# Low-rank delta of the conditioning weight: made in products of 512 columns, partly at the start, and brought back through DRAM

## The chip, the cores and the metric

One core of one Trainium2 chip. The metric is the time of one execution on the device in microseconds (us); lower is better. All data is float32.

## What is computed

The input x has 4096 tokens (32 tiles of 128) of 2048 features. Cut to what matters:

```python
lora_delta = lora_B @ lora_A * 0.5                     # [2048, 64] @ [64, 2048]
cb = codebook / max(|codebook|); scale = exp(scale_log)  # one scale per 128 inputs
normalized = (weight + lora_delta).reshape(O, I // 128, 128) / scale
idx = searchsorted((cb[:-1] + cb[1:]) * 0.5, normalized)  # codebook of 32
w_eff = (cb[idx] * scale).reshape(O, I) + lora_delta
cond = x @ w_eff.T
ffn = cond @ W_base.T + b_base + 2 * mixed(cond) @ B_w.T   # mixed: 8 experts of rank 16, softmax routing
out = x + ffn
```

## The kernel before

**Tiling.** The kernel multiplies the two big weights first: for each block b of 128 input features (16 of them) it makes the row block of G = w_eff.T @ [W_base, A_w, router_w].T, adds the identity, and then multiplies x by G. The width is 2072 columns, cut in five chunks (384, 384, 384, 512, 408). Blocks come in groups of 2, 3, 4, 4 and 3. A group g has two stages: weights(g), which makes its rows of G in 80 slots (for group 0 this is the startup), and tokens(g), 32 tiles of x by five chunks, summed over groups in DRAM (part). The last group also does the routing and the output.

**Quantizing.** A weight block is done in two halves of 1024 output features, so q = 0 to 31, with b = q // 2 and h = q % 2. For each q: POOL adds the delta to the raw weight and divides by the scale (normalise, L924 and L927). Of the 31 thresholds, 25 are units: ACT makes a mask (L678), DVE adds it times its step (L814); six are spare ones (ACT L688, POOL L938 and L942). DVE's L818 closes the sum, POOL's effective(q) multiplies by the scale and adds the delta again (L947, L949). Later ACT and POOL split the result in a high and a low part (L694, L953).

**The order.** All five engines run the same list of events, walk(). An engine does its part of an event and goes on; it is held only by semaphores, and works strictly in order. units(q) yields ("unit", q, j) for j = 0 to 24. In startup() after j = 7 comes ("rows", q - 1) for q = 1 to 4: PE multiplies the half block q - 1 by eight row tiles of the wide weight (L528, plain float32, two records for a product), and SP loads the row tiles, three ahead (L379). ("x_first", 0) comes after j = 12 of q = 4. tokens_of() and weights_of() interleave the units of later q with chunks and slots: q = 5 to 9 in tokens(0), 10 and 11 in weights(1), 12 to 17 in tokens(1), 18 and 19 in weights(2), 20 to 25 in tokens(2), 26 and 27 in weights(3), 28 to 31 in tokens(3).

**The delta.** lora_B is in SBUF (lb), lora_A comes by 128 columns (la, SP, L374). delta(q, r) makes half of a half block: four products of 128 columns into the four quarters of the one PSUM bank pd (L508), and ACT copies the bank to dl, times 0.5 (L668). PE does delta(q + 1, 0) at j = 3 and delta(q + 1, 1) at j = 6 of q; ACT copies at j = 5 and j = 8. Each product waits until the copy of the last one is done. The two of q = 0 stand ahead of the walk on both engines.

Of the kernel before, what the change touches and what calls it, by code (L numbers as in the profile page):

```python
# [49 lines left out]
PER_RING = tuple(len(range(r, NS, RING)) for r in range(RING))  # L50
HOME = (2, 2, 0, 0, 1, 1)
RELEASED = (NS - 4, NS - 2, NS)

COMPUTE = (
# [4 lines left out]
)  # L59
LOADS = (  # L60
    "sl", "lb", "cb", "id", "la0", "la1", *(f"w{r}" for r in range(RAW)), "r0", "r1", "r2",
    *(f"k{r}" for r in range(RING)), "x0", "x1", "x2", "pi0", "pi1", "pi2", "po0", "po1", "po2", "os0", "os1", "os2",
    "bw", "bb", "cr",
)
# [90 lines left out]
class Room:  # L155
    def __init__(self, nc, ctx):
        self.nc = nc
        self.top = -(-nc.sbuf_base // 32) * 32
        raw = [self.space(H * 4) for _ in range(RAW)]
        self.wr = [self.put(f"wr{r}", at, H) for r, at in enumerate(raw)]  # L160
        self.wl = [self.put(f"wl{r}", at, H, F32R) for r, at in enumerate(raw)]
        self.wh = [self.take(f"wh{r}", H, F32R) for r in range(HIGH)]
        self.gh = [self.take(f"gh{k}", DX, F32R) for k in range(NMAX)]
        self.gl = [self.take(f"gl{k}", DX, F32R) for k in range(NMAX)]
        at_x = [self.space(NMAX * 512) for _ in range(3)]
        self.xw = [self.put(f"xw{p}", at, NMAX * 128) for p, at in enumerate(at_x)]
        self.xl = [self.put(f"xl{p}", at, NMAX * 128, F32R) for p, at in enumerate(at_x)]
        self.xh = [self.take(f"xh{p}", NMAX * 128, F32R) for p in range(3)]
        at_p = [self.space(DX * 4) for _ in range(3)]
        self.part = [self.put(f"part{p}", at, DX) for p, at in enumerate(at_p)]  # L170
        self.rows = [self.put(f"rows{p}", at, DX) for p, at in enumerate(at_p)]
        at_k = [at_p[HOME[r]] + (r % 2) * 4096 for r in range(RING)]
        self.kw = [self.put(f"kw{r}", at, 512) for r, at in enumerate(at_k)]
        self.kl = [self.put(f"kl{r}", at, 512, F32R) for r, at in enumerate(at_k)]
        self.kh = [self.put(f"kh{r}", at + 2048, 512, F32R) for r, at in enumerate(at_k)]
        at_dl = self.top
        self.dl = [self.take(f"dl{k}", H) for k in range(2)]
        at_pp = self.top
        self.pp = self.take("pp", H)
        self.tm = self.take("tm", H)  # L180
        self.mk = [self.take(f"mk{k}", H, U8) for k in range(NM)]
        self.mp = [self.take(f"mp{k}", H, U8) for k in range(2)]
        at_lb = self.top
        self.lb = self.take("lb", H)
        self.la = [self.take(f"la{k}", 128) for k in range(2)]
        self.sc = self.take("sc", NB * NB)
        self.rs = self.take("rs", NB * NB)
        self.idn = self.take("idn", 128)
        self.cb = self.take("cb", NC)
        self.cn = self.take("cn", NC)  # L190
        self.u = self.take("u", NC + 1)
        self.th = self.take("th", NJ)
        self.bj = self.take("bj", NJ)
        self.dj = self.take("dj", NJ)
        self.sm = self.take("sm", 2)
        assert self.top <= nc.sbuf_usable_end

        self.tmp = self.put("tmp", at_x[0], 1536)
        self.bw = self.put("bw", at_dl, D)
        self.bs = self.put("bs", at_pp, D, F32R, 96)  # L200
        self.sa = [self.put(f"sa{k}", at_lb + 512 * k, 128, F32R, 96) for k in range(3)]
        self.z = self.put("z", at_lb + 1536, 128)
        self.zt = self.put("zt", at_lb + 2048, 128)
        self.cr = self.put("cr", at_lb + 2560, 96)
        self.ex = self.put("ex", at_lb + 2944, NE)
        self.pe = self.put("pe", at_lb + 2976, NE)
        self.st = self.put("st", at_lb + 3008, 4)

        def bank(name, n=1):
            return ctx.enter_context(nc.psum_tensor(name, [128, n * 512], F32))[:]  # L210

        self.acc = bank("acc", 2)
        self.pd = bank("pd")
        self.m = [bank(f"m{c}") for c in range(NCH)]
        self.pz, self.pm, self.p5 = self.acc[:, 0:512], self.acc[:, 512:1024], self.pd
# [45 lines left out]
def wait_evacuated(e, S, g, t, c):  # L261
    if g == 0 and c in ACT_CHUNKS:
        e.wait_ge(S["ea"], len(ACT_CHUNKS) * t + ACT_CHUNKS.index(c) + 1)
    elif g == 0:
        e.wait_ge(S["ed"], len(DVE_CHUNKS) * t + DVE_CHUNKS.index(c) + 1)
    else:
        e.wait_ge(S["ed"], len(DVE_CHUNKS) * NT + NCH * NT * (g - 1) + NCH * t + c + 1)


def raw_of(q):  # L270
# [90 lines left out]
BOOK_READY = 23  # L361


def sync_program(e, R, S, io, part, out):
    def raw(q):
        b, h = q // 2, q % 2
        if q >= RAW:
            wait_consumed(e, S, q - RAW)
        e.dma_start(R.wr[raw_of(q)], io["w"][b][:, h * H:(h + 1) * H]).then_inc(S[f"w{raw_of(q)}"], 16)

    def lora(b):
        if b >= 2:
            e.wait_ge(S["pd"], 4 * (b - 1))
        e.dma_start(R.la[b % 2], io["la"][:, b * 128:(b + 1) * 128]).then_inc(S[f"la{b % 2}"], 16)  # L374

    def row(r):
        if r >= 3:
            e.wait_ge(S["row"], r - 2)
        e.dma_start(R.rows[r % 3], io["wb"][r % NB]).then_inc(S[f"r{r % 3}"], 16)  # L379
# [42 lines left out]
    e.dma_start(R.cb, io["cb"].partition_broadcast(128)).then_inc(S["cb"], 16)  # L422
    raw(0)
    raw(1)
    lora(1)
    e.dma_start(R.idn, io["id"]).then_inc(S["id"], 16)
    for q in range(2, 2 * N0 + 1):
        raw(q)
    for r in range(3):
        row(r)  # L430
    for ev in walk():
        what, at = ev[0], ev[1:]
        if what == "unit":
            q, j = at
            if j == 0 and 2 * N0 < q + 1 < NQ:
                raw(q + 1)
            if j == 12 and q % 2 == 0 and 2 <= q < NQ - 2:
                lora(q // 2 + 1)
        elif what == "rows":
            for r in range(8 * at[0] + 3, min(8 * at[0] + 11, NB * N0)):  # L440
                row(r)
# [53 lines left out]


def tensor_program(e, R, S):
    def delta(q, r):
        b, h = q // 2, q % 2
        n = 2 * q + r  # L500
        if n == 0:
            e.wait_ge(S["lb"], 16)
        if h == r == 0:
            e.wait_ge(S[f"la{b % 2}"], 16 * (b // 2 + 1))
        if n:
            e.wait_ge(S["dl"], n)
        for k in range(4):
            done = e.matmul(R.pd[:, k * 128:(k + 1) * 128], R.lb[64 * h:64 * h + 64, (4 * r + k) * 128:(4 * r + k + 1) * 128],  # L508
                            R.la[b % 2][64 * h:64 * h + 64, :], start=True, stop=True)
        done.then_inc(S["pd"], 1)  # L510

    def own(b, c):
        return CUT[c] <= b * 128 < CUT[c + 1]
# [100 lines left out]
    def rest(t):  # L614
        if t:
            e.wait_ge(S["e5"], t)
        else:
            e.wait_ge(S["dl"], 2 * NQ)
        low(R.p5, t, NCH - 1, True).then_inc(S["m5"], 1)

    def turn(t):
# [12 lines left out]
            e.wait_ge(S["cr"], 48)  # L634
        e.matmul(R.pm[0:96, 0:128], R.cr, R.zt, start=True, stop=True).then_inc(S["pm"], 1)

    delta(0, 0)
    delta(0, 1)
    for ev in walk():
        what, at = ev[0], ev[1:]  # L640
        if what == "unit":
            q, j = at
            if q + 1 < NQ and j in (3, 6):
                delta(q + 1, (j - 3) // 3)
        elif what == "rows":
            rows(*at)
        elif what == "slot":
            slot(*at)
        elif what == "chunk":
            chunk(*at)  # L650
        elif what == "route":
            route(*at)
        elif what == "turn":
            turn(*at)
        elif what == "mix":
            mix(*at)
        elif what == "last":
            last(*at)
        elif what == "rest":
            rest(*at)  # L660


def scalar_program(e, R, S):
    def delta(q, r):
        e.wait_ge(S["pd"], 2 * q + r + 1)
        if q >= 2 and r == 0:
            e.wait_ge(S["we"], q - 1)
        e.activation(R.dl[q % 2][:, r * 512:(r + 1) * 512], R.pd, ACT.Copy, scale=0.5).then_inc(S["dl"], 1)  # L668

    def unit(q, j):  # L670
        k, w = NV * q + j, R.wr[raw_of(q)]
# [78 lines left out]
        for k in (0, 32, 64):  # L750
            e.activation(R.sa[t % 3][k:k + NR, :], R.pm[k:k + NR, 0:128], ACT.Copy).then_inc(S["mh"], 1)

    delta(0, 0)
    delta(0, 1)
    for ev in walk():
        what, at = ev[0], ev[1:]
        if what == "unit":
            q, j = at
            unit(q, j)
            if q + 1 < NQ and j in (5, 8):  # L760
                delta(q + 1, (j - 5) // 3)
        elif what == "rows_out":
            rows_out(*at)
        elif what == "split":
# [36 lines left out]
def vector_program(e, R, S):  # L801
# [73 lines left out]
    for ev in walk():  # L875
# [19 lines left out]
        elif what == "split" and at[0] == NQ - 1:  # L895
            e.wait_ge(S["we"], NQ)
            e.memset(R.bw, 0.0).then_inc(S["bw0"], 1)
            e.wait_ge(S["pd"], 2 * NQ)
            e.memset(R.cr, 0.0).then_inc(S["cr0"], 1)
        elif what == "slot" and at == (LAST, 20):  # L900
            e.wait_ge(S["bshi"], 1)
# [15 lines left out]
def gpsimd_program(e, R, S):  # L917
    def normalise(q):
        w, d = R.wr[raw_of(q)], R.dl[q % 2]
        e.wait_ge(S[f"w{raw_of(q)}"], 16 * (q // RAW + 1))  # L920
        for r in range(2):
            part = slice(512 * r, 512 * r + 512)
            e.wait_ge(S["dl"], 2 * q + r + 1)
            e.tensor_tensor(w[:, part], w[:, part], d[:, part], ALU.add).then_inc(S["wg"], 1)  # L924
        e.wait_ge(S["wg"], 2 * q + 2)
        e.wait_ge(S["es"], SCALE_FIRST if q < 2 else SCALE_READY)
# [39 lines left out]
                        ALU.subtract).then_inc(S["xl"], 1)  # L966

    def clear():
        e.wait_ge(S["pd"], 2 * NQ)
        for k in range(3):  # L970
            e.memset(R.sa[k].bitcast(F32), 1.0).then_inc(S["s1"], 1)
        e.wait_ge(S["s1"], 3)
# [41 lines left out]

def build(nc, io, out):
    part = nc.dram_tensor("part", [NT, 128, DX], F32, kind="Internal").ap()
    with ExitStack() as ctx:
        R = Room(nc, ctx)
        S = {name: ctx.enter_context(nc.semaphore(f"s_{name}")) for name in COMPUTE}
        S.update({name: ctx.enter_context(nc.semaphore(f"d_{name}")) for name in LOADS})  # L1020
        with nc.Block() as block:
            @block.sync
            def _(e):
                sync_program(e, R, S, io, part, out)

            @block.scalar
            def _(e):
# [45 lines left out]
```

## Time and profile before

| | |
|---|---|
| median of 3 runs | 2537.79 us (2536.51 to 2541.07) |
| the profiled execution | 2540.63 us, span 2538.8 us |
| granted TensorE clock, mean | 0.981 |
| DMA | 461.64 MB, mean 182 GB/s |

The profile is of one execution; times in it count from the start of its span. PE is the matmul part of TensorE and PEld its weight load, DVE VectorE, ACT ScalarE, POOL GpSimd, SP the queue that issues DMAs. A row of a timeline gives the start, the duration, the engine, the line, the operation, output and inputs, and in brackets the idle time of the engine before it and what ended it. L508 is line 508 of the kernel.

### The profile page before, as it was taken

The numbers are of one execution on the slowest core, as the hardware profiler recorded it, in microseconds if no ns is written. First come the engines' busy times: TensorE is split into PE (matmuls) and PEld (weight loads), VectorE is DVE, ScalarE is ACT, GpSimd is POOL, SyncE is SP. The second block draws the span as 40 slices with busy tenths as digits, with TensorE's granted clock in tenths as the row PEclk, the third lists the DMA queues.
The fourth block names the chain that finished last, engine by engine and source line by source line (L and its number), as shares of the span: only waits on it lengthen the run. The fifth ranks groups of instructions, "written<-read, shape, count | busy, mean of one in ns | idle before, by whom it ended". The sixth has DMA issues, their size and how long they took to land.

```text
span 2538.8 us, 32166 instructions
## 1 busy us (share of the span) xinstructions
PE 2371.1 (93%) x12160; PEld 2176.6 (86%) x12160; DVE 1560.8 (61%) x1960; ACT 1499.9 (59%) x1902; POOL 1523.9 (60%) x1062
## 2 busy tenths in 40 slices
PE   1887888889999999999999999999999989999999
PEld 1445777878999989899999989899999989899998
DVE  7996999544899964347777744435566631044444
ACT  6996999666888856666666636654445414311111
POOL 4875888688687877866666646864444436501010
PEclk9988999989999999999999999999999999999999
DMA  2563454434677753345555642335555544456665
GB/s 105 199 213 123 176 184 163 164 100 124 225 285 265 275 210 88 103 140 212 210 213 208 218 151 86 103 125 210 214 215 208 210 156 131 154 199 236 237 236 200
DMA packets 123375, 461.64 MB, mean 182 GB/s; under 512 B 14242, under 2 KB 61602, under 8 KB 82210
## 3 DMA queue, kind: packets, MB, share of 16 engines
q1 hardware_dynamic: 123220, 459.59, 51.6%
q8 instruction: 96, 1.57, 0.2%
q14 instruction: 59, 0.48, 0.1%
HBM read 290.19 MB, written 169.35 MB: 181 GB/s over the span
## 4 chain that ended last, share of the span: by engine, by line
PE 75%; DVE 10%; POOL 7%; ACT 3%; issue 3%; DMA 2%; SPq 0%; DVEq 0%; POOLq 0%; ACTq 0%
PE m L571 17%; PE m L572 17%; PE m L573 17%; DVE acc L814 8%; PE m L555 7%; PE m L557 7%; PE m L556 7%; PE pd L508 2%; ACT mk L678 2%; POOL pp L942 1%; DMA kw<-in_wb 1%; POOL tm L938 1%; PE m L601 1%; POOL kl L959 1%; ACT mp L688 1%
## 5 line engine op out<-in xcount | busy, mean ns | idle before, releaser
L814 DVE SCALAR_TENSOR_TENSOR acc<-mk,dj,acc 128x1024 f32<-128x1024 uint8 x800 | 1026.4, 1283 | 340.6 <-ACT mk L678 229.0
L678 ACT ACTIVATE mk<-wr,bj 128x1024 uint8<-128x1024 f32 x800 | 904.0, 1142 | 233.4 <-DVE acc L814 219.1
L571 PE MATMUL m<-gh,xh 128*128 128x384 f32 (+2 forms) x2560 | 912.8, 357 | 45.7 <-POOL xl L965 19.1
L572 PE MATMUL m<-gl,xh 128*128 128x384 f32 (+2 forms) x2560 | 903.0, 353 | 0.0
L573 PE MATMUL m<-gh,xl 128*128 128x384 f32 (+2 forms) x2560 | 900.7, 352 | 0.0
L571 PEld LDWEIGHTS m<-gh,xh 128*128 128x128 f32 x2560 | 484.4, 189 | 80.1 <-POOL xl L965 23.7
L573 PEld LDWEIGHTS m<-gh,xl 128*128 128x128 f32 x2560 | 484.1, 189 | 23.2
L572 PEld LDWEIGHTS m<-gl,xh 128*128 128x128 f32 x2560 | 484.8, 189 | 20.3
L555 PE MATMUL m<-kh,wh 128*128 128x384 f32 (+2 forms) x1120 | 402.5, 359 | 40.5 <-POOL kl L959 35.3
L959 POOL TENSOR_TENSOR kl<-kw,kh 128x384 fp32r<-128x384 f32 (+2 forms) x320 | 340.7, 1085 | 165.9 <-ACT kh L699 165.4
L836 DVE TENSOR_TENSOR part<-m,part 128x384 f32<-128x384 f32 (+2 forms) x480 | 280.5, 586 | 242.7 <-PE m L573 242.1
L557 PE MATMUL m<-kh,wl 128*128 128x384 f32 (+2 forms) x1120 | 397.4, 355 | 0.0
L556 PE MATMUL m<-kl,wh 128*128 128x384 f32 (+2 forms) x1120 | 397.2, 355 | 0.0
L942 POOL TENSOR_TENSOR pp<-pp,tm 128x1024 f32<-128x1024 f32 x160 | 383.2, 2395 | 13.4
L965 POOL TENSOR_TENSOR xl<-xw,xh 128x384 fp32r<-128x384 f32 (+2 forms) x160 | 171.3, 1072 | 350.4 <-ACT xh L719 349.6
L699 ACT ACTIVATE kh<-kw 128x384 fp32r<-128x384 f32 (+2 forms) x320 | 172.4, 546 | 318.3 <-DMA kw<-in_wb 317.1
L938 POOL TENSOR_SCALAR tm<-mp,dj 128x1024 f32<-128x1024 uint8 x192 | 215.4, 1122 | 173.5 <-ACT mp L688 169.4
L555 PEld LDWEIGHTS m<-kh,wh 128*128 128x128 f32 x1120 | 214.6, 192 | 58.7 <-POOL kl L959 40.8
L556 PEld LDWEIGHTS m<-kl,wh 128*128 128x128 f32 x1120 | 214.5, 192 | 9.7
L557 PEld LDWEIGHTS m<-kh,wl 128*128 128x128 f32 x1120 | 214.1, 191 | 9.8
L688 ACT ACTIVATE mp<-wr,bj 128x1024 uint8<-128x1024 f32 x192 | 217.9, 1135 | 0.0
L822 DVE TENSOR_TENSOR gl<-m,gh 128x384 fp32r<-128x384 f32 (+2 forms) x80 | 45.2, 588 | 203.3 <-ACT gh L714 203.3
(84 smaller groups left out, 1479.9 us busy)
## 6 DMA issues: line engine op xcount, KB each, us to landing
part<-part SPq DMA_DIRECT2D x256, 1036.0 KB, 4.8
kw<-in_wb SPq DMA_DIRECT2D x192, 192.0 KB, 2.4
rows<-in_wb SPq DMA_DIRECT2D x32, 1036.0 KB, 4.8
out<-part SPq DMA_DIRECT2D x32, 1024.0 KB, 3.9
wr<-in_w SPq DMA_DIRECT2D x32, 512.0 KB, 5.8
kw<-in_wb SPq DMA_DIRECT2D x64, 256.0 KB, 2.6
xw<-in_x SPq DMA_DIRECT2D x64, 256.0 KB, 2.9
kw<-in_wb SPq DMA_DIRECT2D x64, 204.0 KB, 2.4
```

The lines of the kernel that those rows point to most:

```text
L555: e.matmul(bank[:, 0:w], high, kh, start=t == 0, stop=False)
L556: e.matmul(bank[:, 0:w], high, kl, start=False, stop=False)
L557: done = e.matmul(bank[:, 0:w], low, kh, start=False, stop=t == NB - 1 and not own(b, c))
L571: e.matmul(R.m[c][:, 0:w], xh, gh, start=k == 0, stop=False)
L572: e.matmul(R.m[c][:, 0:w], xh, gl, start=False, stop=False)
L573: done = e.matmul(R.m[c][:, 0:w], xl, gh, start=False, stop=stop and k == n - 1)
L678: e.activation(R.mk[k % NM], w, ACT.Identity, bias=R.bj[:, j:j + 1], scale=GROW).then_inc(S["mk"], 1)
L688: e.activation(R.mp[k % 2], w, ACT.Identity, bias=R.bj[:, NV + i:NV + i + 1], scale=GROW).then_inc(S["mp"], 1)
L814: e.scalar_tensor_tensor(R.acc, R.mk[k % NM], R.dj[:, j:j + 1], R.acc, ALU.mult, ALU.add).then_inc(S["ac"], 1)
L836: e.tensor_tensor(p, R.m[c][:, 0:width(c)], p, ALU.add).then_inc(S["ed"], 1)
L942: e.tensor_tensor(R.pp, R.pp if i else w, R.tm, ALU.add).then_inc(S["pp"], 1)
L959: e.tensor_tensor(R.kl[r][:, 0:w], R.kw[r][:, 0:w], R.kh[r][:, 0:w].bitcast(F32), ALU.subtract).then_inc(S["gl"], 1)
```

## The change

The delta is no longer made half by half just ahead of its use. A product is now 512 columns wide: delta(n) multiplies one tile of 128 output features of lb by four blocks of lora_A, n = 0 to 63. Its result spans four blocks, so ACT copies it into one of two buffers ds, two products side by side, and SP stores each pair to a DRAM tensor delta (512 KB, runs of 1 KB). SP loads the half block that q + 1 needs at j = 5 of q into dl, and POOL waits for that load. Ahead of the walk PE and ACT do four direct products of the old form (q = 0 and 1) and then delta(0) to delta(15). The other 48 are placed at j = 2, 8, 14 and 20 of q = 1 to 12, on PE and ACT in the same event; from q = 13 on there are none. la and ds lie in space of gh3 and gl3, which only groups of four blocks use.

```diff
+DIRECT = 4
+QUADS = NB // 4
+DU_AT = (2, 8, 14, 20)
...
+def early(q):
+
+    first = 16 + len(DU_AT) * (q - 1)
+    return range(first, first + len(DU_AT)) if 0 < q and first < 16 * QUADS else ()
...
+    def lora(Q):
+        if Q >= 2:
+            e.wait_ge(S["pd"], DIRECT + 16 * (Q - 1))
+        e.dma_start(R.la[Q % 2], io["la"][:, Q * 512:(Q + 1) * 512]).then_inc(S[f"la{Q % 2}"], 16)
...
+    def delta_out(n):
+        Q, ot, p = n // 16, n % 16, n // 2 % 2
+        e.wait_ge(S["dl"], DIRECT + n + 1)
+        e.dma_start(delta[4 * Q:4 * Q + 4, :, (ot - 1) * 128:(ot + 1) * 128].rearrange("b p i -> p b i"),
+                    R.ds[p].rearrange("p (b i) -> p b i", b=4)).then_inc(S[f"ds{p}"], 16)
...
+    def delta_in(q):
+        b, h = q // 2, q % 2
+        pairs = 8 * (b // 4) + 4 * h + 4
+        for p in range(2):
+            e.wait_ge(S[f"ds{p}"], 16 * (pairs // 2))
+        e.wait_ge(S["we"], q - 1)
+        e.dma_start(R.dl[q % 2], delta[b, :, h * H:(h + 1) * H]).then_inc(S[f"dq{q % 2}"], 16)
...
+    lora(1)
+    for n in range(1, 16, 2):
+        delta_out(n)
+    lora(2)
...
+            if j in DU_AT and early(q):
+                n = early(q)[DU_AT.index(j)]
+                if n % 2:
+                    delta_out(n)
+                if n % 16 == 15 and n // 16 + 2 < QUADS:
+                    lora(n // 16 + 2)
+            if j == 5 and 1 <= q < NQ - 1:
+                delta_in(q + 1)
...
+    def direct(h, r):
+        if h == r == 0:
             e.wait_ge(S["lb"], 16)
-        if h == r == 0:
-            e.wait_ge(S[f"la{b % 2}"], 16 * (b // 2 + 1))
...
+            e.wait_ge(S["la0"], 16)
+        else:
+            e.wait_ge(S["dl"], 2 * h + r)
...
         done.then_inc(S["pd"], 1)
...
+    def delta(n):
+        Q, h, ot = n // 16, n % 16 // 8, n % 8 * 128
+        if n % 16 == 0:
+            e.wait_ge(S[f"la{Q % 2}"], 16 * (Q // 2 + 1))
+        e.wait_ge(S["dl"], DIRECT + n)
+        e.matmul(R.pd, R.lb[64 * h:64 * h + 64, ot:ot + 128], R.la[Q % 2][64 * h:64 * h + 64, :],
+                 start=True, stop=True).then_inc(S["pd"], 1)
...
-    delta(0, 0)
-    delta(0, 1)
+    for n in range(DIRECT):
+        direct(n // 2, n % 2)
+    for n in range(16):
+        delta(n)
...
-            if q + 1 < NQ and j in (3, 6):
-                delta(q + 1, (j - 3) // 3)
+            if j in DU_AT and early(q):
+                delta(early(q)[DU_AT.index(j)])
...
+    def delta(n):
+        p, ot = n // 2 % 2, n % 2 * 128
+        e.wait_ge(S["pd"], DIRECT + n + 1)
+        if n >= 4 and n % 2 == 0:
+            e.wait_ge(S[f"ds{p}"], 16 * (n // 4))
+        e.activation(R.ds[p].rearrange("p (b i) -> p b i", b=4)[:, :, ot:ot + 128],
+                     R.pd.rearrange("p (b i) -> p b i", b=4), ACT.Copy, scale=0.5).then_inc(S["dl"], 1)
...
-            if q + 1 < NQ and j in (5, 8):
-                delta(q + 1, (j - 5) // 3)
+            if j in DU_AT and early(q):
+                delta(early(q)[DU_AT.index(j)])
...
-            e.wait_ge(S["dl"], 2 * q + r + 1)
+            if q < 2:
+                e.wait_ge(S["dl"], 2 * q + r + 1)
+            elif r == 0:
+                e.wait_ge(S[f"dq{q % 2}"], 16 * (q // 2))
...
+    delta = nc.dram_tensor("delta", [NB, 128, D], F32, kind="Internal").ap()
```

In the diff, the functions with lora and delta_out, delta_in are SP's; of the two functions delta(n) the first is PE's and the second ACT's.

## Rows read from the trace of the kernel before

**Rows 1.** The page: busy time of each engine, and the chain by engine.
```profile
PE 2371.1 (93%) x12160; PEld 2176.6 (86%) x12160; DVE 1560.8 (61%) x1960; ACT 1499.9 (59%) x1902; POOL 1523.9 (60%) x1062
PE 75%; DVE 10%; POOL 7%; ACT 3%; issue 3%; DMA 2%; SPq 0%; DVEq 0%; POOLq 0%; ACTq 0%
```

**Rows 2.** The chain by line: 1100 to 1500 us, then 230 to 470.
```profile
by line: PE m L571 30.8%; PE m L572 30.3%; PE m L573 30.0%; PE pd L508 3.3%; PE m L557 1.9%; PE m L556 1.9%; PE m L555 1.9%
...
by line: DVE acc L814 17.3%; issue 14.9%; ACT mk L678 7.4%; POOL pp L942 6.2%; PE m L571 5.9%; PE m L573 4.9%; PE m L572 4.8%; POOL tm L938 4.6%; POOL xl L965 4.3%; POOL wr L924 4.2%; POOL wl L953 4.0%; POOL wr L949 4.0%; DVE wr L818 3.2%; 
```

**Rows 3.** Busy time by stretch, length, PE, PEld, DVE, ACT, POOL, clock, DMA: tokens(0), (2), (1).
```profile
324.40:369.00 44.60, 39.04 (x196) 35.56 (x196) 41.43 (x45) 41.98 (x54) 36.30 (x24) 0.96 0.47 173
...
1242.00:1301.10 59.10, 59.10 (x318) 55.66 (x317) 45.59 (x52) 39.52 (x40) 38.49 (x23) 1.00 0.59 213
691.40:735.80 44.40, 44.05 (x238) 41.01 (x237) 43.58 (x52) 38.71 (x40) 37.03 (x23) 1.00 0.72 273
```

**Rows 4.** Timeline of DVE, startup: the ends of q = 0, 1, 3, 4.
```profile
25.75 34.72 DVE L814 SCALAR_TENSOR_TENSOR acc<-mk,dj,acc 128x1024 f32<-128x1024 uint8 x25 [4.82 <-ACT acc L682]
60.50 1.28 DVE L818 SCALAR_TENSOR_TENSOR wr<-acc,cn,pp 128x1024 f32<-128x1024 f32 x1
...
97.69 1.28 DVE L818 SCALAR_TENSOR_TENSOR wr<-acc,cn,pp 128x1024 f32<-128x1024 f32 x1
...
174.35 1.28 DVE L818 SCALAR_TENSOR_TENSOR wr<-acc,cn,pp 128x1024 f32<-128x1024 f32 x1
...
211.96 1.29 DVE L814 SCALAR_TENSOR_TENSOR acc<-mk,dj,acc 128x1024 f32<-128x1024 uint8 x1 [17.16 <-ACT mk L678]
...
229.29 1.28 DVE L818 SCALAR_TENSOR_TENSOR wr<-acc,cn,pp 128x1024 f32<-128x1024 f32 x1
```

**Rows 5.** Timeline of PE: a delta half at the high clock, rows(1), rows(3).
```profile
102.88 1.16 PE L508 MATMUL pd<-la,lb 64*128 64x128 f32 x8
...
107.47 29.61 PE L528 MATMUL m<-rows,wr 128*128 128x384 f32 x80
...
184.93 30.13 PE L528 MATMUL m<-rows,wr 128*128 128x384 f32 x80
```

**Rows 6.** Timeline of ACT: a delta half is copied, q = 2.
```profile
105.63 0.58 ACT L668 ACTIVATE dl<-pd 128x512 f32<-128x512 f32 x1
```

**Rows 7.** Timeline of ACT: before the first unit.
```profile
10.07 0.60 ACT L668 ACTIVATE dl<-pd 128x512 f32<-128x512 f32 x1 [2.16 <-PE pd L508]
21.49 1.15 ACT L678 ACTIVATE mk<-wr,bj 128x1024 uint8<-128x1024 f32 x1 [10.82 <-POOL wr L927]
```

**Rows 8.** Timeline of all engines: the first delta products on PE.
```profile
5.23 2.04 PE L508 MATMUL pd<-la,lb 64*128 64x128 f32 x8 [5.23 <-DMA la<-in_la]
...
7.96 2.07 PE L508 MATMUL pd<-la,lb 64*128 64x128 f32 x8 [0.69 <-ACT dl L668]
```

**Rows 9.** Groups of PE by form: 73 to 77 us, 77.7 to 80.5 us.
```profile
L528 PE MATMUL m<-rows,wr 128*128 128x512 f32 x2 | 1.7, 956 | 0.0
...
L528 PE MATMUL m<-rows,wr 128*128 128x512 f32 x2 | 1.0, 592 | 0.0
```

**Rows 10.** Stretches of two delta products; PEclk is the third number from the end.
```profile
182.90:185.00 2.10, 2.07 (x9) 1.85 (x9) 2.00 (x2) 2.05 (x2) 1.86 (x2) 0.50 0.11 39
...
102.90:104.00 1.10, 1.10 (x9) 0.94 (x8) 1.08 (x1) 1.10 (x2) 1.10 (x2) 1.00 0.97 301
```

**Rows 11.** The page: loads of raw weight, KB each, median us to landing.
```profile
wr<-in_w SPq DMA_DIRECT2D x32, 512.0 KB, 5.8
```

**Rows 12.** Timeline of POOL: the end of effective(1).
```profile
101.03 2.36 POOL L949 TENSOR_TENSOR wr<-wr,dl 128x1024 f32<-128x1024 f32 x1
```

**Rows 13.** Waits of ACT, 230 to 470 us: us in total, times, longest.
```profile
ACT part L725 <- PE m L573: 27.0, 16, 7.3
```

**Rows 14.** Waits, from 470 us on.
```profile
ACT dl L668 <- PE pd L508: 42.1, 17, 5.1
```

**Rows 15.** Groups, 640 to 2070 us: the delta products.
```profile
L508 PE MATMUL pd<-la,lb 64*128 64x128 f32 x304 | 44.8, 289 | 0.0
```

More of the change, by code:

```diff
@@ L60 @@
 LOADS = (
-    "sl", "lb", "cb", "id", "la0", "la1", *(f"w{r}" for r in range(RAW)), "r0", "r1", "r2",
+    "sl", "lb", "cb", "id", "la0", "la1", "ds0", "ds1", "dq0", "dq1", *(f"w{r}" for r in range(RAW)), "r0", "r1", "r2",
     *(f"k{r}" for r in range(RING)), "x0", "x1", "x2", "pi0", "pi1", "pi2", "po0", "po1", "po2", "os0", "os1", "os2",
@@ L163, in __init__ @@
         self.gh = [self.take(f"gh{k}", DX, F32R) for k in range(NMAX)]
+        at_gh, at_gl = self.top - DX * 4, self.top + (NMAX - 1) * DX * 4
         self.gl = [self.take(f"gl{k}", DX, F32R) for k in range(NMAX)]
+        self.la = [self.put(f"la{k}", at_gh + 2048 * k, 512) for k in range(2)]
+        self.ds = [self.put(f"ds{k}", at_gl + 4096 * k, H) for k in range(2)]
         at_x = [self.space(NMAX * 512) for _ in range(3)]
@@ L184, in __init__ @@
         self.lb = self.take("lb", H)
-        self.la = [self.take(f"la{k}", 128) for k in range(2)]
         self.sc = self.take("sc", NB * NB)
@@ L361, with sync_program @@
 BOOK_READY = 23
-def sync_program(e, R, S, io, part, out):
+def sync_program(e, R, S, io, part, delta, out):
     def raw(q):
@@ L369, in raw @@
         e.dma_start(R.wr[raw_of(q)], io["w"][b][:, h * H:(h + 1) * H]).then_inc(S[f"w{raw_of(q)}"], 16)
[L371 to L374, printed above, removed]
+    def lora(Q):
[14 more added lines that the diff above has]
+        e.dma_start(R.dl[q % 2], delta[b, :, h * H:(h + 1) * H]).then_inc(S[f"dq{q % 2}"], 16)
     def row(r):
@@ L424, in sync_program @@
     raw(1)
-    lora(1)
     e.dma_start(R.idn, io["id"]).then_inc(S["id"], 16)
@@ L436, in sync_program @@
                 raw(q + 1)
-            if j == 12 and q % 2 == 0 and 2 <= q < NQ - 2:
-                lora(q // 2 + 1)
+            if j in DU_AT and early(q):
[6 more added lines that the diff above has]
+                delta_in(q + 1)
         elif what == "rows":
@@ L497, in tensor_program @@
 def tensor_program(e, R, S):
[L498 to L501, printed above, removed]
+    def direct(h, r):
+        if h == r == 0:
             e.wait_ge(S["lb"], 16)
-        if h == r == 0:
-            e.wait_ge(S[f"la{b % 2}"], 16 * (b // 2 + 1))
-        if n:
-            e.wait_ge(S["dl"], n)
+            e.wait_ge(S["la0"], 16)
+        else:
+            e.wait_ge(S["dl"], 2 * h + r)
         for k in range(4):
-            done = e.matmul(R.pd[:, k * 128:(k + 1) * 128], R.lb[64 * h:64 * h + 64, (4 * r + k) * 128:(4 * r + k + 1) * 128],
-                            R.la[b % 2][64 * h:64 * h + 64, :], start=True, stop=True)
+            ot = (4 * r + k) * 128
+            done = e.matmul(R.pd[:, k * 128:(k + 1) * 128], R.lb[64 * h:64 * h + 64, ot:ot + 128],
+                            R.la[0][64 * h:64 * h + 64, 0:128], start=True, stop=True)
         done.then_inc(S["pd"], 1)
+    def delta(n):
[5 more added lines that the diff above has]
+                 start=True, stop=True).then_inc(S["pd"], 1)
     def own(b, c):
@@ L617, in rest @@
         else:
-            e.wait_ge(S["dl"], 2 * NQ)
+            e.wait_ge(S["dl"], DIRECT + 16 * QUADS)
         low(R.p5, t, NCH - 1, True).then_inc(S["m5"], 1)
@@ L663, in scalar_program, with direct @@
 def scalar_program(e, R, S):
[L664 to L668, printed above, removed]
+    def direct(h, r):
+        e.wait_ge(S["pd"], 2 * h + r + 1)
+        e.activation(R.dl[h][:, r * 512:(r + 1) * 512], R.pd, ACT.Copy, scale=0.5).then_inc(S["dl"], 1)
+    def delta(n):
[5 more added lines that the diff above has]
+                     R.pd.rearrange("p (b i) -> p b i", b=4), ACT.Copy, scale=0.5).then_inc(S["dl"], 1)
     def unit(q, j):
@@ L751, in mix @@
             e.activation(R.sa[t % 3][k:k + NR, :], R.pm[k:k + NR, 0:128], ACT.Copy).then_inc(S["mh"], 1)
-    delta(0, 0)
-    delta(0, 1)
+    for n in range(DIRECT):
+        direct(n // 2, n % 2)
+    for n in range(16):
+        delta(n)
     for ev in walk():
@@ L897, in vector_program @@
             e.memset(R.bw, 0.0).then_inc(S["bw0"], 1)
-            e.wait_ge(S["pd"], 2 * NQ)
+            e.wait_ge(S["pd"], DIRECT + 16 * QUADS)
             e.memset(R.cr, 0.0).then_inc(S["cr0"], 1)
@@ L968, in clear @@
     def clear():
-        e.wait_ge(S["pd"], 2 * NQ)
+        e.wait_ge(S["pd"], DIRECT + 16 * QUADS)
         for k in range(3):
@@ L1023, in _ @@
             def _(e):
-                sync_program(e, R, S, io, part, out)
+                sync_program(e, R, S, io, part, delta, out)
             @block.scalar
```

## Prediction, made before the changed kernel was run

> **What bounds the kernel now.** I read the page first. TensorE (PE) is busy 93% of the span and holds 75% of the chain that ended last; DVE, ACT and POOL stand near 60% each [rows 1]. Such shares average over stages, so I then asked for the chain by stretch. From 1100 to 1500 us it is PE and nothing else, 3.3% of it the delta products of L508; but from 230 to 470 us, the tokens of group 0, the quantizing of the weights leads (DVE L814, ACT L678, POOL) and PE has a small part [rows 2]. Busy times by stretch say the same: PE 59.1 of 59.1 us in one q of tokens(2), 44.05 of 44.4 in tokens(1) with DVE at 43.58, and in group 0 DVE 41.4, ACT 42.0 and PE 39.0 of 44.6 [rows 3]. The kernel thus has two parts. Up to about 470 us the chain of units decides: ACT makes the mask, DVE adds it. Later PE decides. PE works in program order, so a delay of the first part moves the end one to one, while PE time saved later comes off the end.
>
> Startup is the stretch to look at. DVE ends its q with L818. The ends for q = 0, 1, 3 and 4 (start plus 1.28) are 61.8, 99.0, 175.6 and 230.6 us [rows 4]: q = 1 took 37.2, q = 2 and 3 together 76.6, q = 4 55.0. The 25 units of q = 0 take 34.7 us [rows 4], 1.39 each. The long last one has a wait of 17.2 us on ACT [rows 4], which stood at j = 12 for the first x tile: in its list SP has that load behind the row loads, and these wait for PE. Meanwhile PE does rows(q-1), eight row tiles that need about 30 us: 29.6 and 30.1 us in two of the four passes [rows 5]. They run beside the units, because nothing that ACT needs during a q is queued behind them: both delta products of a q stand ahead (j = 3 and 6; rows at j = 7), and ACT picks them up two units later.
>
> **The change, part by part.**
>
> (a) Ahead of the first unit. Before, ACT needed only two evacuations, and from 10.7 us sat idle for 10.8 us until the scales were ready and its first mask began at 21.5 us [rows 7]. Now 4 direct and 16 wide products come first, each one waiting for the evacuation of the last since there is a single bank, pd. A direct one has the old form: products start at 5.2 and 8.0 us, one each 2.75 us [rows 8]; four end at 5.2 + 11.0 = 16.2. A wide one is two records of 512 columns. No row shows it for delta; the nearest is the row product of 512 columns in two records: a mean of 956 ns at the low clock and 592 at the high one [rows 9], so 1.9 or 1.2 us. The hand-over costs 0.7 us, the idle time of PE between products [rows 8]. A wide product thus takes 2.6 or 1.9 us. Which clock? The granted clock is not recorded that early, but eight narrow records take 2.04 us there, as at a granted 0.50 (1.2 GHz), against 1.16 us at 1.00 (2.4 GHz) [rows 5, 8, 10]. PE stayed low while busy three quarters of the time over the products shown, and the wide ones keep it as busy, so I take 2.6: 16 x 2.6 = 41.6, and ACT is free at 57.8 instead of 21.5, +36 us. At the high clock it is 16 x 1.9 = 30.4, end 46.6, +25. The stores: a ds buffer is needed again three products after its store goes out, 3 x 2.6 - 0.6 = 7.2 us; the nearest row for 512 KB is 5.8 us to landing [rows 11]. Just hidden; at the high clock it has 5.1 us and would hold the chain back, so +25 to +45 is the range. The ends of (a) lie on the chain whole: DVE and POOL have nothing else to do.
>
> By the Trainium skill, TensorE: Matmul & The Clock Gate, section "What's actually happening", the clock follows how busy the array has been of late, and sustained work brings it to 2.4 GHz. Read strictly, forty microseconds of this would rise and (a) would be the +25 case, the sum 11 us less; the products of rows 8 do not show it.
>
> (b) The wait that is new. DU_AT puts deltas at j = 2, 8, 14, 20, on PE and on ACT in the same event. In startup rows(q-1) is yielded after j = 7, so PE does the delta of j = 8 after all eight row tiles, and ACT, in order, cannot make the mask of j = 9 until it has evacuated that delta. Behind it stand DVE's units 9 to 24, POOL's spares and normalise(q+1), and so the next q. Let T be the end of L818 of q-1. effective(q-1) ends at T + 4.4 (101.03 + 2.36 against 99.0) [rows 12], the rows take 30 us, to T + 34.5; the product at the high clock 1.1, the evacuation 0.6 [rows 6], the mask 1.1 [rows 7]: T + 37.3. Then 16 units x 1.39 = 22.3 and L818 1.3: T + 61. Four periods (q = 1 to 4) of 61 are 244 against 168.8 (230.6 - 61.8): **+75 us**. Within it the x stall of q = 4 is gone: SP's row loads and the load of x are done by T + 43, about when ACT comes to j = 12. In SP's queue delta_in at j = 5 waits for effective(q-1), T + 4.4, ahead of the row loads of j = 7, the first of which needs a row product done at T + 10: no cost. delta_out of j = 8 waits there until T + 37, and only x stands behind it. Bounds: 65 (rows take 28) to 82 (rows slowed by the other loads, ACT with its six spare masks behind for a few us).
>
> (c) Group 0, q = 5 to 9. Four evacuations per q instead of two: 10 more x 0.5 = 5 us of an ACT that is 94% busy. Also 20 waits at PE's heels, since the two-unit lead is gone. The nearest row is ACT's wait for PE at L725: 16 times, 27.0 us, 1.7 each [rows 13]; 20 x 1.7 = 34 is the upper end, nothing the lower. PE is mostly level with ACT here, so I take a quarter, about 10: **+15**, 0 to 39.
>
> (d) q = 10 to 12, 12 products in the same event. ACT's waits for delta after 470 us: 17 times, 42.1 us [rows 14], 2.5 each, upper end 30; most is slack. SP's delta_out stands ahead of kw loads in weights(1), with three slots of lead. **+7**, 0 to 30.
>
> (e) q = 13 on: no products and no evacuations. PE spends 44.8 us on 304 records from 640 us on [rows 15], 38 halves of 1.18 each; 36 of them go, 42.5 us. In tokens(2) and (3) all of it is on the chain; in tokens(1), 10 halves, DVE stands within 1 us of PE per q [rows 3], so about half goes: **-35**, from -42 to -25.
>
> (f) DMA: 16.8 MB more written, about 15.7 MB more read on 462. delta_in goes out at j = 5 and POOL needs it at j = 9: over 5.6 us against 5.8 [rows 11], but in group 0 and later POOL reaches normalise later still, and in startup the stall of (b) covers it. Lost cover would cost 1 to 2 us per q. Zero.
>
> Sum: 36 + 75 + 15 + 7 - 35 = **+98 us**. The profiled execution took 2540.6 us (span 2538.8); 2638.6. The median of the runs is 2.8 lower: **2636**.
>
> **The rivals.**
> 1. As forecast, both ACT stalls real. Lowest: 25 + 65 + 0 + 0 - 42 = +48 (2586); highest 45 + 82 + 39 + 30 - 25 = +171 (2709). 88%; its middle 2590 to 2695.
> 2. The new waits reach much further: each delta store or delta_in blocks SP's order and starves kw, x or part in the groups, one more stall of about 2.5 us for each of the 48 placed products: +120 on top, 2756. For it: one queue, waits on other engines in it. Against: loads run two tiles or three slots ahead. 5%.
> 3. The startup stall of (b) is not there, because PE gets the j = 8 product done before the rows: then the sum is 98 - 75 = +23, 2559. Against: PE is in order and the product is behind the rows in its list. 3%.
> 4. Faster: stall absent as in 3, prologue at the high clock (+25), group 0 and weights(1) absorb the rest at nothing, all of L508 gained: 25 - 42 = -17, 2521. It decides for faster if rows(q-1) are over by about T + 15, when ACT comes to j = 8, so in some 10 us; they take 30 [rows 5]. 3%.
> 5. That the change does little: the two sides cancel within 0.2%, 5 us. 1%.
>
> **How the numbers follow.** Faster 0.03, same 0.01, slower 0.96. A measurement of this kernel tells 0.2% from no change. The range 2590 to 2695 leaves out rivals 2 to 5 and the far ends of the first.
>
> **What would show it.** Right: first mask of ACT near 58 us; in q = 1 to 4 an idle time of ACT of about 20 us before the second wide evacuation, ended by PE's delta product, with rows just ahead of it; DVE's L818 about 61 us apart; group 0 beginning its tokens about 110 us later; q from 13 on about 2.2 us shorter in tokens(2). Wrong: rows that end before ACT's j = 8, or a prologue under 45 us; or SP waits that end after the loads are due in weights(1).

## The result: slower by 4.8%

The changed kernel takes 2661.5 us (median of 4 runs, 2652.8 to 2666.5) against 2538.6 of the kernel before on the same chip: a ratio of 1.048, 95% interval 1.0451 to 1.0509. The forecast was 2636. The profiled execution took 2660.9 us, its span is 2659.1, which is 120.3 longer than before.

The page of the changed kernel, to be set beside [rows 1]; then its waits from 814 to 1065 us, where q = 13 to 17 lie (us in total, times, longest):

```profile
PE 2396.6 (90%) x11808; PEld 2144.1 (81%) x11808; DVE 1563.8 (59%) x1960; ACT 1500.2 (56%) x1906; POOL 1524.0 (57%) x1062
PE 71%; POOL 7%; ACT 7%; DVE 6%; DMA 6%; issue 2%; SPq 0%; DVEq 0%; POOLq 0%; ACTq 0%
...
ACT xh L767 <- DMA xw<-in_x: 59.8, 23, 4.5
...
POOL wr L977 <- DMA dl<-delta: 20.9, 5, 4.9
```

DMA has 6% of the chain where it had 2%. All shares say little until the span is cut at the ends of the q. The table does that: each number is the distance, in one trace, between two ends of DVE's closing instruction (L818 before, L868 after; as in [rows 4]). "mask" is the start of ACT's first mask, "tail" what follows the end of q = 31.

| us | mask | q0 | q1-3 | q4 | q5-9 | q10-12 | q13-17 | q18-31 | tail | span |
|---|---|---|---|---|---|---|---|---|---|---|
| before | 21.5 | 40.3 | 113.9 | 54.9 | 228.1 | 232.7 | 222.6 | 1132.3 | 492.6 | 2538.8 |
| after | 61.3 | 40.3 | 187.6 | 61.5 | 229.3 | 234.6 | 248.7 | 1099.6 | 496.2 | 2659.1 |
| e1 | 61.2 | 40.3 | 120.4 | 58.2 | 232.3 | 231.3 | 250.0 | 1094.0 | 496.4 | 2584.2 |
| e2 | 38.7 | 40.3 | 188.7 | 61.6 | 229.4 | 234.7 | 247.3 | 1096.2 | 495.5 | 2632.3 |
| e3 | 60.9 | 40.3 | 189.8 | 61.7 | 229.3 | 237.2 | 238.4 | 1097.2 | 495.9 | 2650.8 |
| e4 | 21.6 | 40.3 | 113.8 | 53.5 | 227.8 | 233.0 | 233.4 | 1131.3 | 492.7 | 2547.4 |
| e5 | 61.0 | 40.3 | 120.0 | 58.1 | 232.8 | 232.9 | 222.4 | 1096.0 | 496.2 | 2559.4 |
| e6 | 22.2 | 40.3 | 113.8 | 54.6 | 231.6 | 234.5 | 256.4 | 1097.4 | 497.0 | 2547.8 |
| e7 | 22.6 | 40.3 | 113.8 | 54.8 | 231.6 | 234.6 | 230.6 | 1097.1 | 493.7 | 2519.1 |
| e8 | 21.8 | 40.3 | 113.9 | 54.7 | 227.6 | 233.3 | 222.6 | 1131.3 | 495.7 | 2541.2 |
| e9 | 24.6 | 40.3 | 113.8 | 54.7 | 234.3 | 235.0 | 223.1 | 1097.1 | 497.0 | 2520.0 |

The first two lines hold the result: +39.8 ahead of the first mask, +73.7 and +6.6 in q = 1 to 4, nearly nothing in q = 5 to 12, +26.1 in q = 13 to 17, -32.7 from q = 18 on, +3.6 in the tail.

**Ahead of the first mask.** ACT in the changed kernel: start, duration, operation, idle before it.

```profile
8.31 0.60 ACT L708 ACTIVATE dl<-pd 128x512 f32<-128x512 f32 x1 [6.29 <-PE pd L540]
...
22.17 0.60 ACT L715 ACTIVATE ds<-pd 128x512 f32<-128x512 f32 x1 [2.16 <-PE pd L549]
24.93 0.60 ACT L715 ACTIVATE ds<-pd 128x512 f32<-128x512 f32 x1 [2.16 <-PE pd L549]
...
60.79 0.60 ACT L715 ACTIVATE ds<-pd 128x512 f32<-128x512 f32 x1 [2.16 <-PE pd L549]
61.29 1.14 ACT L726 ACTIVATE mk<-wr,bj 128x1024 uint8<-128x1024 f32 x1
```

The copies come 2.76 us apart to the last, and the first mask stands right behind the twentieth. PE gives the other half, a direct product (eight narrow records) and a wide one:

```profile
14.48 2.07 PE L540 MATMUL pd<-la,lb 64*128 64x128 f32 x8 [0.69 <-ACT dl L708]
...
20.06 2.07 PE L549 MATMUL pd<-la,lb 64*128 64x512 f32 x2 [0.69 <-ACT ds L715]
```

**The stall in startup.** PE, ACT and DVE in q = 1 of the changed kernel, and the next end:

```profile
106.04 29.71 PE L568 MATMUL m<-rows,wr 128*128 128x384 f32 x80 [42.46 <-POOL wr L1002]
135.68 1.12 PE L549 MATMUL pd<-la,lb 64*128 64x512 f32 x2
...
111.03 1.15 ACT L726 ACTIVATE mk<-wr,bj 128x1024 uint8<-128x1024 f32 x1 [0.24 <-DVE acc L864]
136.84 0.60 ACT L715 ACTIVATE ds<-pd 128x512 f32<-128x512 f32 x1 [24.66 <-PE pd L549]
137.34 1.14 ACT L726 ACTIVATE mk<-wr,bj 128x1024 uint8<-128x1024 f32 x1
...
100.30 1.28 DVE L868 SCALAR_TENSOR_TENSOR wr<-acc,cn,pp 128x1024 f32<-128x1024 f32 x1
...
161.40 1.28 DVE L868 SCALAR_TENSOR_TENSOR wr<-acc,cn,pp 128x1024 f32<-128x1024 f32 x1
```

To be read in this order: all 80 row records are on PE ahead of the product of j = 8; ACT made the mask of that j at 111.0 and then stood 24.7 us; q = 1 took 61.1 us.

### The profile page after: what moved, and what is told of

It reads as the page before. It is cut to its first block, busy times and chain, and to the rows that moved or that the text cites. A ratio compares the mean times of both kernels' runs of the same rounds, so it can differ in the third digit from the quotient of the medians.

```text
span 2659.1 us, 31535 instructions
## 1 busy us (share of the span) xinstructions
PE 2396.6 (90%) x11808; PEld 2144.1 (81%) x11808; DVE 1563.8 (59%) x1960; ACT 1500.2 (56%) x1906; POOL 1524.0 (57%) x1062
## 4 chain that ended last, share of the span: by engine, by line
PE 71%; POOL 7%; ACT 7%; DVE 6%; DMA 6%; issue 2%; SPq 0%; DVEq 0%; POOLq 0%; ACTq 0%
PE m L611 14%; PE m L612 14%; PE m L613 14%; PE m L595 7%; PE m L597 6%; PE m L596 6%; DVE acc L864 5%; PE m L568 4%; DMA part<-part 4%; ACT mk L726 3%; PE pd L549 2%; POOL pp L995 2%; ACT mp L736 1%; POOL kl L1012 1%; POOL tm L991 1%
## 5 line engine op out<-in xcount | busy, mean ns | idle before, releaser
L611 PEld LDWEIGHTS m<-gh,xh 128*128 128x128 f32 x2560 | 486.5, 190 | 120.4 <-POOL xl L1018 45.6
L568 PE MATMUL m<-rows,wr 128*128 128x384 f32 (+2 forms) x320 | 118.8, 535 | 79.7 <-POOL wr L1002 64.5
```

The lines of the kernel that those rows point to most:

```text
L611: e.matmul(R.m[c][:, 0:w], xh, gh, start=k == 0, stop=False)
```

## Experiments

### e1: the products ahead of the rows

```diff
-DU_AT = (2, 8, 14, 20)
+DU_AT = (1, 3, 5, 7)
```

> The changed kernel with its four placed products at j = 1, 3, 5 and 7 instead of 2, 8, 14 and 20: all ahead of the row tiles on PE, nothing else. My theory (ACT is held at j = 8 because PE has the product behind rows(q-1)): ACT's waits of 20 to 26 us for L549 in q = 1 to 4 go, PE now needs about 10 us of paced products and 30 of rows for a q, so L868 comes every 41 us or so in q = 1 to 3 instead of 61 to 65, and q = 4 gets back part of its wait for x (55 to 60). Sum for q = 1 to 4 near 180 instead of 249, the time about 2660 - 68 = 2592. Rival (the stall comes from the traffic or the waits of the stores and loads through DRAM, which stay the same): the periods stay at 61 and the time within 5 us of 2660. Nothing changes for q = 13 to 17 by either.

Measured: 2585.5 us (4 runs, ratio to before 1.0178, 1.0161 to 1.0195), 76 us less than the changed kernel. q = 1 to 4 take 178.6 us. PE in q = 1 of e1:

```profile
109.46 2.07 PE L549 MATMUL pd<-la,lb 64*128 64x512 f32 x2 [0.69 <-ACT ds L715]
111.46 30.39 PE L568 MATMUL m<-rows,wr 128*128 128x384 f32 x80
141.78 1.12 PE L549 MATMUL pd<-la,lb 64*128 64x512 f32 x2
```

The traffic through DRAM is the same, only the place in PE's list is another, and the periods of 61 to 65 us of q = 1 to 3 become 37 to 43. ACT's longest wait for a product in startup falls from 26.3 us to 3.9. The stall came from the order. In q = 4 a wait of 18.5 us for the first x tile is back, as expected in part. What is left in q = 2 and 3 (40.3 and 42.9 instead of 37.2 and 39.5) is PE, as expected: paced products plus 30 us of rows.

### e2: half the prologue

```diff
+AHEAD_OF_WALK = 8
+DU_FIRST = (1, 4, 7, 10, 13, 16, 19, 22)
...
-    for n in range(16):
+    for n in range(AHEAD_OF_WALK):
         delta(n)
...
+    if q == 0:
+        return range(AHEAD_OF_WALK, 16)
```

> The changed kernel with 8 wide products ahead of the walk instead of 16; products 8 to 15 stand in q = 0 at j = 1, 4, 7, 10, 13, 16, 19 and 22. My theory (the prologue lies on the chain whole, 2.76 us for a product at the low clock): the first mask comes at 61.3 - 8 x 2.76 = 39.2 us; in q = 0 ACT has 8 x 0.5 = 4 us more to do and PE is idle, so the end of q = 0 falls from 101.6 to 80 to 84, and the time by 18 to 22 us to about 2640. Rival (the stores of the pairs pace it, not PE and ACT): the products left take longer each, or delta_in of q = 2 lands too late, and less than 10 us are gained.

Measured: 2634.0 us (ratio 1.0371, 1.0352 to 1.0389), 27.6 less than the changed kernel by the medians, 26.8 by the spans, more than the 18 to 22 expected. The first mask comes at 38.7, 22.6 earlier, and q = 0 takes 40.3 us as ever: the eight copies moved there cost nothing, where I had allowed 4 us for them: the copies fit beside DVE's units, which set the pace of q = 0. The prologue is on the chain whole and the stores don't pace it. The other 4 us lie in q = 13 to 19 (-5.0) and are no more than runs of the changed kernel differ by.

### e3 and e4: what makes q = 13 to 17 slow

e3 leaves out the return of the delta from q = 13 on; POOL adds what dl still holds. e4 is the kernel before with an extra load. Both are single runs.

```diff
-            if j == 5 and 1 <= q < NQ - 1:
+            if j == 5 and 1 <= q < 12:
                 delta_in(q + 1)
...
-            elif r == 0:
+            elif r == 0 and q <= 12:
```

```diff
+            if j == 5 and 12 <= q < 17:
+                if q > 12:
+                    e.wait_ge(S["xt"], 16 * (q - 12))
+                e.dma_start(R.xt, io["w"][0][:, 0:H]).then_inc(S["xt"], 16)
```

> The changed kernel without the loads of the delta for the half blocks 13 to 31: POOL adds what dl holds then, so the weights from q = 13 on are not the right ones; all other work is the same. Theory A (the 512 KB read per q, in SP's list and on the DMA queues, is what makes q = 13 to 17 in tokens(1) 49 to 51 us long instead of 44.5): their sum falls from 248.8 to 222 to 230 us. Theory B (SP fell behind during q = 12, where delta stores and loads come together, and the loop of store, part and x loads cannot catch up): the sum stays above 240, since x loads stay late. In tokens(2) and weights(2) and (3) neither expects more than 3 us.

> The kernel before with one extra load of 512 KB into an unused place for each of q = 12 to 16, at j = 5, where the changed kernel has its load of the delta; nobody reads it. Theory A (the extra read alone tips tokens(1)): q = 13 to 17 take 235 to 250 us instead of 222.5, with ACT waiting for x. Theory B (the seed lies in q = 12's delta stores and products, or in POOL's wait for the load): 222 to 226 us, and the time stays within 5 us of 2540.

Measured: in e3 q = 13 to 17 take 238.4 us, between the two forecasts: q = 13 44.5, the rest 47.6 to 50.2, though not one byte of delta is read there. In e4 they take 233.4, again between the forecasts: 44.5, 44.5, 45.6, 49.4, 49.4. The last extra load of e4 goes out in q = 16, and q = 17 is still slow. Neither theory holds alone. The 512 KB load can start it: it is all that e4 adds to the kernel before. In e3 it starts without that load, some 20 us after the last delta store of q = 12. What starts it there is not isolated: e3 still has the four products, their copies and the two stores of q = 12, and, like the changed kernel, no products behind them. Once started it goes on without any of these to the end of q = 17, for 23 tiles in e3 and 6 in e4. ACT waits for x tiles 59.8 us in q = 13 to 17 of the changed kernel, 46.2 in e3 and 28.9 in e4, and in the kernel before not at all. SP in tokens(1), the kernel before, where L412 stores part, L407 loads it and L398 loads x; then e4 near its end (L414, L409, L400), where no extra load is in flight:

```profile
736.42 0.32 SPq L412 DMA_DIRECT2D part<-part  x1
740.32 0.32 SPq L407 DMA_DIRECT2D part<-part  x1
...
741.85 0.33 SPq L398 DMA_DIRECT2D xw<-in_x  x1
745.62 0.33 SPq L412 DMA_DIRECT2D part<-part  x1
```

```profile
867.04 0.33 SPq L409 DMA_DIRECT2D part<-part  x1
867.42 0.43 SPq L400 DMA_DIRECT2D xw<-in_x  x1
868.02 0.32 SPq L414 DMA_DIRECT2D part<-part  x1
876.33 0.32 SPq L409 DMA_DIRECT2D part<-part  x1
```

Before, the store goes out 3.8 us after the x load and the next part load follows it by 3.9 us, which is when the store has landed. In e4 all three go out within a microsecond and SP then stands 8.3 us for the store, which has 1 MB of part and the x tile ahead of it. The x tile of the next load is late by that, PE by the x tile. An estimate from these rows says why the lag is not made up: 8.3 us for the store and 1.0 for the three issues are 9.3 us for a tile, where 44.5 us for a q of five tiles leave 8.9. The landing times in q = 13 to 17 (medians of 24 or 25 DMAs, of 5 for the delta):

| us to landing | store of part | load of part | load of x | load of delta |
|---|---|---|---|---|
| before | 4.6 | 4.9 | 4.3 | - |
| after | 8.5 | 5.9 | 6.7 | 7.0 |
| e3 | 8.4 | 6.1 | 6.4 | - |
| e4 | 8.2 | 5.5 | 6.2 | - |
| e5 | 5.7 | 5.1 | 5.3 | 5.7 |
| e9 | 4.9 | 5.0 | 5.3 | 5.8 |

### e5 and e8: another place in SP's list

e5 is e1, e8 the kernel before, each with this edit in SP's part of ("chunk", g, t, 0):

```diff
+                if g and 2 <= t < NT - 1:
+                    load_part(g, t + 1)
                 if t + 2 < NT:
                     load_x(g, t + 2)
                 if t:
                     store_part(g, t - 1)
-                    if g and t + 2 < NT:
-                        load_part(g, t + 2)
```

> The kernel of e1 (products at j = 1, 3, 5, 7) with the load of part, in groups 1 to 3, issued one tile later and ahead of the x load and the store, so that SP no longer stands until the store of the tile before has landed. Theory A (a closed loop: SP waits for the landing of a store that shares the DMA queues with the part and x loads issued just ahead of it, so x comes late, so PE, so the next store; once tipped it stays): q = 13 to 17 fall from 250 to 222 to 232 us and ACT's waits for x (82 us before 1200 us) mostly go; the whole is about 2560 to 2565. Theory B (the DMA engines simply have too much to move with the extra 512 KB): the sum stays above 240.

> The kernel before with the later part load alone, as the control for e5 and e7. Both theories: within 0.2% of 2540, since its tokens(1) never waits for x; if it gains more than 5 us the loop of SP was already a cost before.

Measured: e5 2561.2 us (one run), q = 13 to 17 in 222.4, 44.5 each. e8 2538.9 (10 runs, ratio 0.9997, 0.9988 to 1.0007). The numbers are those of theory A, but the reason given in the expectation is not right, and the trace of e5 says so:

```profile
822.54 0.32 SPq L432 DMA_DIRECT2D part<-part  x1
822.91 0.43 SPq L423 DMA_DIRECT2D xw<-in_x  x1
824.71 0.32 SPq L437 DMA_DIRECT2D part<-part  x1
830.87 0.32 SPq L432 DMA_DIRECT2D part<-part  x1
```

SP still stands 6.2 us for the store. Written out, the order of store, part and x loads is the same as before the edit; a part load is only named at the next chunk event. What did move is everything that SP does for units between two chunk events: the raw weight, the delta load and the delta store stood between the part load and the x load, and now stand right behind the store, ahead of the wait. The 512 KB are moved while SP waits anyway, and x has only part ahead of it. That this is why it helps is argued from the list and not tested by itself. What e5 does show is this: the same bytes in another order cost nothing in q = 13 to 17 (ACT has no wait for x there), and it is not a matter of too many bytes. That the slow form keeps itself going is what e3 and e4 show, for the old order. In the new one it need not: e9 has a tile with x issued at 738.0 us and the store at 738.7, which lands in 7.8, and four tiles later a store lands in 4.6 again. Why the new order recovers is open.

### e6, e7 and e9: only what pays

The three leave half blocks 0 to 7 as in the kernel before and make 48 wide products for q = 8 to 31. e7 is e6 with the edit of e5; e9 is e7 with all products ahead of q = 12.

```diff
+NDIRECT = 8
+PE_AT, ACT_AT = (3, 6), (5, 8)
+WIDE_AT = {5: (11, 14, 17, 20), 6: (11, 14, 17, 20), 7: (1, 4, 7, 10, 13, 16, 19, 22),
+           **{q: (2, 8, 14, 20) for q in range(8, 16)}}
```

```diff
+WIDE_AT = {**{q: (9, 12, 15, 17, 20, 23) for q in (5, 6)}, 7: (1, 4, 7, 10, 13, 16, 19, 22),
+           **{q: (2, 6, 10, 14, 18, 22) for q in (8, 9)}, **{q: (1, 4, 7, 10, 13, 16, 19, 22) for q in (10, 11)}}
```

> A mix: half blocks 0 to 7 get their delta as in the kernel before (products at j = 3 and 6, copies at 5 and 8), and only 48 wide products are made, 4 in q = 5 and in q = 6, 8 in q = 7, 4 in each of q = 8 to 15, returned through DRAM for q = 8 on. No prologue, no product behind the rows. My accounting: startup as before (first mask 21.5, q = 1 to 4 168.8), q = 5 to 9 longer by 0 to 8 (ACT has up to 8 more copies in q = 7), q = 13 to 17 longer by 15 to 30 as in the changed kernel, q from 18 on and shorter by 33: about 2540 to 2555. Rival (the copies do not fit into ACT's time in group 0): q = 5 to 9 longer by 15 or more, 2560 and above.

> e6 with the later part load of e5. Theory A: q = 13 to 17 take 220 to 228 us, so what is left is the gain from q = 18 on, about 30 us: 2505 to 2520, faster than the kernel before. Theory B: q = 13 to 17 stay near 245 and the time near that of e6.

> e7 with its 48 wide products all placed ahead of q = 12: 6 each in q = 5, 6, 8 and 9, 8 each in q = 7, 10 and 11. In e7 the three q of tokens(1) that still had four products took 47.2 us each, the two without 44.5. My theory (ACT, DVE and PE are all nearly full in tokens(1), so that is the worst place for products, while group 0 takes them at about 1 us per q): q = 13 to 17 fall from 230.6 to 222.5, q = 5 to 9 rise by 0 to 4, and the time is 2515 to 2521. Rival (the gain in tokens(1) is given back in group 0 and weights(1)): within 3 us of 2524.

Measured: e6 2546.8 us (8 runs, ratio 1.0031, 1.0019 to 1.0043), within its forecast, though q = 13 to 17 take 256.4 us, 34 more than before and not 15 to 30. e7 2524.2 (4 runs, 0.9937, 0.9922 to 0.9952): the edit of e5 alone takes 22.6 us off e6 (q = 13 to 17: 230.6 us instead of 256.4), which bears out the single run of e5 with several. It is 4 us above its forecast because three q of tokens(1) with products take 47.2 us each, which I had put at nothing; e9 2516.5 (4 runs, 0.9897, 0.9881 to 0.9914). e9 beats both kernels, by 1.0% and 5.4%. Its q = 13 to 17 take 223.1 and the price is 6 us in q = 5 to 9, 2 in q = 10 to 12 and, in this trace, 3 ahead of the first mask, against before. Its page:

```profile
PE 2362.3 (94%) x11872; PEld 2137.5 (85%) x11872; DVE 1560.5 (62%) x1960; ACT 1500.7 (60%) x1902; POOL 1525.6 (61%) x1062
```

## Why the prediction came out as it did, step by step

The direction and the two large terms were right. The measured total, +120, is 22 above the sum of 98, and that difference is made of misses of both signs. That the number came so near is in part luck: (c) and (d) were priced 19 us too high, and that hides most of the 26 us of (f), which had been put at nothing. What happened in (f) is the mechanism of rival 2, delta transfers in SP's queue that make x late, but in one stage only and at 26 us instead of 120. (Rival 3 should read 2561, 2538 + 23, and not 2559; nothing hangs on it.)

(a) The prologue, forecast +36, measured +39.8. The low clock was the right choice: sixteen wide products in a row took 2.07 us each, as eight narrow records take at a granted 0.50 [rows 10], with 0.69 between them. The trace records no granted clock that early; from 146 to 160 us, at a granted 0.50, a wide product takes 2.07 us too. I had 1.9 for a product from the row records, 2.7 us too little over sixteen; the larger la load delayed the start from 5.2 to 6.2 us. Read strictly, the rule of the Trainium skill, TensorE: Matmul & The Clock Gate, section "What's actually happening", that sustained work brings the clock to 2.4 GHz, would have had it rise in that time. By the durations it did not in the 43 us of the wide products, with a PE that is busy 2.07 of every 2.76 us.

(b) The stall, forecast +75, measured +80.3; e1 shows its cause. The steps for q = 1 hold within 0.4 us: with T = 101.6 the rows begin at T + 4.5, end at T + 34.2, DVE goes on at T + 36.9 (138.5) and ends the q at T + 61.1, forecast 61. Most of the miss is q = 3, 65.0 us: there rows(2) begin only at T + 8.6, since PE waits for DVE to empty the banks of block 0 (rows_out(0) at j = 4), a wait that the forecast left out by taking all four q as alike. PE's rows are what the q waits for, so their late start moves its end.

(c) Group 0, forecast +15, measured +1.2. The wait row of L725 was the wrong neighbour: ACT waited for wide products only 3.7 us in five times from 351 to 580 us, PE being ahead of it. And ten more copies did not show in the periods (44.8 against 44.6). ACT's 94% busy was not the bound of that stretch.

(d) q = 10 to 12, forecast +7, measured +1.9.

(e) q = 13 on, forecast -35. From q = 18 it is -32.7 by the table; tokens(2) went from 59.1 to 56.6 us per q. The tail took 3.6 back. PE is busy 480.0 us there at a granted clock of 0.98, against 476.6 at 0.99 before; e8, which has no change of the delta, has 495.7 and 0.98 too, and e7, which has it, 493.7 and 0.99. So in these traces the tail goes with the granted clock and not with the delta. The share that I expected of tokens(1), some -5, does not exist: in e5, where nothing of (f) is left, PE is busy 214.6 us of q = 13 to 17 instead of 222.4 and they still take 222.4 us, with DVE busy 218.4.

(f) The traffic, forecast zero, measured +26 in q = 13 to 17: the step that failed. I had compared bytes and the landing time of the load with the time until POOL needs it, and looked only at that one transfer. POOL did wait for it (20.9 us). But some 16 of the 26 us stay when the load is left out (e3, 238.4 against 222.6 us): they come from the transfers beside it, x and part, and from SP, which stands on a landing once per tile. Tokens(1) moved 273 GB/s already [rows 3], the most of any stage shown; that row was in my hand and should have named the place. e4 shows that an extra load of this size starts it, e3 that it also starts and goes on without the load, e5 and e7 that the place in SP's list decides.

Taken together: with (a), (b) and (f) undone, e9 keeps nearly all of (e), and that is the gain that the change has in it.

## What to carry to other kernels

On an engine that works in order, a new instruction costs what stands ahead of it, not what it takes: look at every engine's own list, at the event where it is put, for the longest thing between the producer's place and the consumer's. A queue that waits for landings is such an engine too: place extra transfers right behind the one that it is about to wait for, and look at the stage that moves most bytes, not at the mean. Work moved out of a stage bound by the matrix engine into one that isn't pays, if it is neither put ahead of the first use nor behind the long work of that stage.

## What the runs showed of the hardware that I had not expected

- A product of 512 columns in two records takes as long as four of 128 in eight: 2.07 and 2.07 us at the low clock, 1.12 and 1.16 at the high one. Six records and six weight loads fewer bought nothing at the low clock and 0.04 us at the high one; all the gain came from where the products stand.
- A store of 512 KB in runs of 1 KB landed in 3.2 us (median of 32), less than the load of 512 KB from rows of 4 KB with 5.7 us (30). I had priced it by the load. Most of these stores fell where little else was moved: the two in tokens(1) took 8.0 and 6.9 us, the loads there 6.4 to 7.2.
- A store of 1 MB landed in 4.6 us (median of 25, kernel before) where it mostly went out some microseconds behind the x load, and in 8.5 (median of 25, changed kernel) where it was issued mostly within a microsecond or so behind a part load and an x load. In e3 this slow form kept itself going for 23 tiles with no transfer of the delta.
